# Eight rounding steps of GpSimd moved from ahead of a split of row maxima to behind it

## The chip, the cores and the metric

One core of one Trainium2 chip runs the whole program. The metric is the time of one execution on the device in microseconds, as the median of three runs. Five engines take part: TensorE (PE in the rows, PEld for its weight loads), VectorE (DVE), ScalarE (ACT), GpSimd (POOL) and SyncE (SP), which only issues transfers here.

## What is computed

The input is x with 4 x 1024 tokens of 128 features. The output is x plus an attention block plus a feed-forward block, both of which read the same layer norm of x:

```python
xn = _layernorm(x, axis=-1)
x = x + attn(xn, Wq, bq, Wk, bk, Wv, bv, Wo, bo) + ffn(xn, w_gate, w_up, w_down)
# attn: 16 heads of 8 features, a linear bias per head on the scores, softmax over 1024 keys
# ffn:
gate = fp4_linear(x, w_gate)
y = fp4_linear(x, w_up)
h = jax.nn.silu(gate) * y
return fp4_linear(h, w_down)
```

`fp4_linear` rounds both its operands to a grid of eight magnitudes in blocks of 16 values, each block scaled by its largest magnitude over 6. The feed-forward width is 352.

## The kernel before

**Tiling.** The attention goes in 32 halves m: 4 batches x 4 quads of heads x 2 halves of the queries. A half takes 8 units, so the main loop has 256 units U (and 16 more that drain it). In a unit, TensorE makes four score products for the exponentials (`score`, L1247, 128 keys x 512 queries each) and, for a later half, four score products the other way round (`half_chunk`, L1228, 128 queries x 512 keys each), out of which VectorE takes the row maxima (L1079). The maxima run ahead of the exponentials by `LEAD` = 22 chunks of two such products. ScalarE takes the exponentials (L863); TensorE multiplies them by the values (`value_product`, L1258).

**The way of the maxima.** When the last chunk of a half has been reduced, VectorE joins the two halves of each row into `neg_max` (L1085). GpSimd splits it into two bf16 parts (`max_parts`, L759 and L760) and raises `parts_max_ok` (L762). TensorE transposes the parts (`turn`, L1236), ScalarE keeps them (L869), SyncE writes them to DRAM and reads them into the operand rows of the scores (L536, L539), and the scores of the half begin three units after the transposition. The transposition of half m stands at the end of unit 8m - 3 (`turn_unit`), and GpSimd's split at the head of the same unit. VectorE's `neg_max` for it comes at the end of unit 8m - 4.

**The rounding.** The feed-forward block goes in 16 pairs p of token tiles, one every 15 units. Its places are given by a small planner (`plan`), and the rounding of its hidden values is tied to `up`, the unit of the pair's last `up` product. It is split into steps:

- VectorE: block maxima, scales (`up` + 3) and their inverses (`up` + 4, L1063)
- GpSimd, `scale_to_grid` at `up` + 5: two multiplications (L633, 128 x 704, and L635, 128 x 256), then `z_ok`
- VectorE, `powers` at `up` + 6, second half of the unit: waits for `z_ok`, one operation (L1068), then `pow_ok`
- GpSimd, `add_power` at `up` + 7: waits for `pow_ok`, two operations (L644 and L645, 128 x 960)
- GpSimd, `take_power` at `up` + 9: one operation (L650)
- GpSimd, `scale_back` at `up` + 10: two operations (L661 writes `hq`, L669 writes `xq`), then `quant_ok`

TensorE transposes `hq` (job `hT`, L1288) 13 or 14 units after `up` and again later, after a wait for `quant_ok`.

**Order.** Each engine has its own program, in which all of this is written in the order of units; an engine does nothing out of that order. Inside a unit GpSimd's order is: the split of the maxima, the bias, the attention result (`context`, L749), jobs of the feed-forward block (`swish` L722 and L723, `hidden` L728, `add_down` L735, `add_wo` L741), the steps of the rounding, the normalisation and the three-part split of q and k. TensorE's banks for row maxima are three, so it can be at most three products ahead of VectorE; its banks for everything that ScalarE empties are four.

Of the kernel before, what the change touches and what calls it, by code (L numbers as in the profile page):

```python
# [74 lines left out]
HALVES = 2 * B * QUADS  # L75
# [5 lines left out]
def turn_unit(m):  # L81
    return (16 * m + 15 - LEAD) // 2 + 1
# [25 lines left out]
def head(U, j):  # L108
# [6 lines left out]
FROM_XT = {("gate", 0): 2, ("gate", 1): 4, ("up", 0): 7, ("up", 1): 9, ("hT", 0): 23, ("hT", 1): 26,  # L115
           ("down", 0): 28, ("down", 1): 31}
ROUNDED = 13


def norm_unit(b):  # L120
    return 1 if b == 1 else 60 * b - 59


def parts_unit(g):
    return 60 * (g // 2 - 1) + 16 + 15 * (g % 2)


def plan():
# [17 lines left out]
    for p in range(NP):  # L146
        start = FFN_FIRST + FFN_STEP * p
        U = put(start, "xT", p)
        for kind, t in FROM_XT:
            U = U + (ROUNDED if (kind, t) == ("hT", 0) else 1)  # L150
            if p + 1 < NP or kind in ("gate", "up"):
# [74 lines left out]
def attn_ffn(nc, x, wq, bq, wk, bk, wv, bv, wo, bo, wg, wu, wd, out):  # L226
    with ExitStack() as ctx:
# [352 lines left out]
        def _(pool):  # L580
# [48 lines left out]
            def scale_to_grid(job):  # L629

                pool.wait_ge(inv_ok, job + 1)
                w, values = (W_END, w_all) if job == 0 else (PI, hid)
                mark(nc.gpsimd.tensor_tensor(blocks(zb[:, 0:w]), blocks(values[:]), spread(inv[:, 0:w // BLK]), ALU.mult))  # L633
                for c, p in x_cols(job):
                    mark(nc.gpsimd.tensor_tensor(blocks(zb[:, c:c + PW]), blocks(pair_x(p)),  # L635
                                                 spread(inv[:, c // BLK:(c + PW) // BLK]), ALU.mult))
                settle()
                pool.sem_inc(z_ok, 1)

            def add_power(job):  # L640
                w = job_cols(job)
                z, m = zb[:, 0:w], mb[:, 0:w]
                pool.wait_ge(pow_ok, job + 1)
                link(nc.gpsimd.tensor_scalar(m, m, 1.0, ROUND, ALU.max, ALU.mult))  # L644
                link(nc.gpsimd.tensor_tensor(z, z, m, ALU.add))  # L645

            def take_power(job):
                w = job_cols(job)
                z, m = zb[:, 0:w], mb[:, 0:w]
                link(nc.gpsimd.tensor_tensor(z, z, m, ALU.subtract))  # L650

            def scale_back(job):

                if job == 0:
                    mark(nc.gpsimd.tensor_tensor(blocks(w_all[:]), blocks(zb[:, 0:W_END]), spread(sc[:, 0:W_END // BLK]),
                                                 ALU.mult))
                else:
                    n = PI // BLK
                    if job >= 2:
                        pool.wait_ge(st_full, ST["hT", job - 2, 1] + 1)  # L660
                    mark(nc.gpsimd.tensor_tensor(  # L661
                        hq[:, :, 0:I].rearrange("p t (n k) -> p t n k", k=BLK),
                        zb[:, 0:PI].rearrange("p (t n k) -> p t n k", t=2, k=BLK),
                        sc[:, 0:n].rearrange("p (t n) -> p t n", t=2).unsqueeze(3).to_broadcast([P, 2, n // 2, BLK]),
                        ALU.mult))
                for c, p in x_cols(job):
                    if p >= 2:
                        pool.wait_ge(st_full, ST["xT", p - 2] + 1)
                    mark(nc.gpsimd.tensor_tensor(blocks(xq[p % 2][:]), blocks(zb[:, c:c + PW]),  # L669
                                                 spread(sc[:, c // BLK:(c + PW) // BLK]), ALU.mult))  # L670
                settle()
                pool.sem_inc(quant_ok, 1)
# [12 lines left out]
            def add_bias(b):  # L685

                pool.wait_ge(bo_ok, 1)
                for i in range(2):
                    group = x_s[:, b * S + i * GW:b * S + (i + 1) * GW].rearrange("p (t e) -> p t e", e=E)
                    ins = nc.gpsimd.tensor_tensor(group, group, bo_s[:].unsqueeze(1).to_broadcast([P, GT, E]), ALU.add)  # L690
                ins.then_inc(xb_ok, 1)
# [27 lines left out]
            def swish(p):  # L719

                pool.wait_ge(st_free, ST["gate", p, 1] + 1)
                link(nc.gpsimd.tensor_scalar(tanh_s[:], tanh_s[:], 1.0, None, ALU.add))  # L722
                link(nc.gpsimd.tensor_tensor(gate_s[:], tanh_s[:], gate_s[:], ALU.mult))  # L723

            def hidden(p, t):
                half = slice(t * I, (t + 1) * I)
                pool.wait_ge(st_free, ST["up", p, t] + 1)
                link(nc.gpsimd.tensor_tensor(hid[:, half], gate_s[:, half], up_s[:, half], ALU.mult))  # L728
                pool.sem_inc(hid_ok, 1)

            def add_down(p, t):
                to = x_s[:, p * PW + t * P:p * PW + (t + 1) * P]
                pool.wait_ge(st_free, ST["down", p, t] + 1)
                pool.wait_ge(xb_ok, p // 4 + 1)
                link(nc.gpsimd.tensor_tensor(to, to, down_s[:, t * P:(t + 1) * P], ALU.add))  # L735
                pool.sem_inc(down_ok, 1)

            def add_wo(hb, i):
                to = o_s[hb % 2][:, i * PW:(i + 1) * PW]
                pool.wait_ge(st_free, ST["wo", hb, i] + 1)  # L740
                nc.gpsimd.tensor_tensor(to, to, x_s[:, hb * GW + i * PW:hb * GW + (i + 1) * PW], ALU.add).then_inc(out_ok, 1)  # L741

            def context(m):
                b, quad, half = m // 8, m // 2 % QUADS, m % 2
                pool.wait_ge(pv_r_ok, m + 1)
                heads = pv_s[:].rearrange("p (t h c) -> p t h c", h=4, c=32)
                if b >= 2 and quad == 0 and half == 0:
                    pool.wait_ge(st_full, ST["ctxT", 2 * b - 3] + 1)
                nc.gpsimd.tensor_tensor(  # L749
                    ctx_s[b % 2][:, 4 * half:4 * half + 4, 32 * quad:32 * quad + 32].rearrange(  # L750
                        "p t (h d) -> p t h d", d=D), heads[:, :, :, 0:D],
                    pv_r[:].rearrange("p (t h) -> p t h", h=4).unsqueeze(3).to_broadcast([P, 4, 4, D]),
                    ALU.mult).then_inc(ctx_ok, 1)

            def max_parts(m):
                pool.wait_ge(max_ok, m + 1)
                if m >= 2:
                    pool.wait_ge(st_full, ST["turn", m - 2] + 1)
                link(nc.gpsimd.tensor_copy(neg_parts[m % 2][:, 0:16], neg_max[m % 2][:]))  # L759
                link(nc.gpsimd.tensor_tensor(neg_parts[m % 2][:, 16:32], neg_max[m % 2][:], neg_parts[m % 2][:, 0:16],  # L760
                                             ALU.subtract))
                pool.sem_inc(parts_max_ok, 1)  # L762
# [8 lines left out]
            for U in range(NU + 2 * KT):  # L771
                b, u = divmod(U, QUADS * UNITS)
                for m in range(1, HALVES):
                    if U == turn_unit(m):
                        max_parts(m)
                if u == 2 and b < B:
                    add_bias(b)
                for job in JOBS.get(U - 1, ()):
                    if job[0] == "pvT":
                        context(job[1])  # L780
                for job in JOBS.get(U - 1, ()):
                    if job[0] == "gate" and job[2] == 1:
                        swish(job[1])
                    elif job[0] == "up":
                        hidden(job[1], job[2])
                    elif job[0] == "down":
                        add_down(job[1], job[2])
                    elif job[0] == "wo" and job[1] + 1 < NG:
                        add_wo(job[1], job[2])
                for p in range(NP):  # L790
                    up = AT["up", p, 1]
                    if U == up + 5:
                        scale_to_grid(p + 1)
                    if U == up + 7:
                        add_power(p + 1)
                    if U == up + 9:
                        take_power(p + 1)
                    if U == up + 10:
                        scale_back(p + 1)
                for g in range(2, NG):  # L800
                    if U == norm_unit(g // 2):
                        normalize(g)
                    if U == parts_unit(g):
                        three_parts(g, 0, "q")
                    if U == parts_unit(g) + 2:
                        three_parts(g, 1, "k")
# [600 lines left out]
```

## Time and profile before

| | |
|---|---|
| median of 3 runs | 804.6 us (804.46 to 805.57) |
| the profiled execution, its own time | 801.33 us |
| its span, first to last instruction | 799.5 us |
| TensorE busy | 92% |
| VectorE busy | 89% |
| ScalarE busy | 83% |
| GpSimd busy | 53% |
| granted TensorE clock, mean | 0.97 |

A unit takes some 2.8 to 3 us. Three engines are nearly full and hand banks to each other, so the table alone doesn't say what sets the time: the waits and the chain of work have to be read at the places of the change.

### The profile page before, as it was taken

To read this page: it belongs to the slowest core of one execution; us is meant where nothing else is said; L and a number is where in the kernel's file an instruction comes from. 1 tells how busy PE (TensorE), PEld (TensorE's weight loads), DVE (VectorE), ACT (ScalarE), POOL (GpSimd) and SP (SyncE) were. 2 spreads that over 40 slices of the span, in tenths; PEclk is the share of its full clock that TensorE was granted. 3 is DMA by queue.
4 is the path that set the end of the run, shared out by engine and by line. 5 is a ranking of instruction groups with operands and counts; after the bars stand their busy time and mean duration, and the time that the engine had idled before them with its cause. 6 is when DMAs were issued, how large, how long until landed. Compare 5 with 4: busy or idle time off the path is not lost.

```text
span 799.5 us, 14573 instructions
## 1 busy us (share of the span) xinstructions
PE 736.7 (92%) x4951; PEld 218.3 (27%) x4951; DVE 711.9 (89%) x1304; ACT 661.4 (83%) x1366; POOL 427.0 (53%) x449
## 2 busy tenths in 40 slices
PE   6399998999899999999999999999899999999987
PEld 2012222222223222322222332322222322222223
DVE  8998899999899899999999899999898999999930
ACT  4107988888888988898889989898888898898896
POOL 5792157563545658581736656662627372634351
PEclk9657999999999999999999999999999999999999
DMA  6730002041101020060101001240100100000000
GB/s 183 219 73 2 2 3 81 2 134 27 41 1 41 2 81 2 23 151 15 42 1 42 3 33 50 93 93 2 41 2 22 34 3 1 15 2 2 2 2 27
DMA packets 33042, 31.90 MB, mean 40 GB/s; under 512 B 4456, under 2 KB 26856, under 8 KB 32968
## 3 DMA queue, kind: packets, MB, share of 16 engines
q1 hardware_dynamic: 32840, 30.86, 14.3%
q8 instruction: 40, 0.66, 0.4%
q14 instruction: 34, 0.28, 0.1%
q10 hardware_dynamic: 128, 0.10, 0.0%
HBM read 15.91 MB, written 15.04 MB: 39 GB/s over the span
## 4 chain that ended last, share of the span: by engine, by line
PE 63%; DVE 25%; ACT 5%; POOL 4%; issue 3%; DMA 0%; POOLq 0%; SPq 0%; ACTq 0%; DVEq 0%
PE pv L1258 23%; PE mx L1228 23%; DVE neg_half L1079 20%; ACT probs L863 3%; PE low L1281 3%; PE low L1275 2%; PE low L1307 2%; PE low L1296 2%; PE low L1208 2%; POOL zb L645 1%; PE low L1288 1%; PE low L1322 1%; POOL mb L644 1%; DVE am L1048 1%; PE low L1204 1%
## 5 line engine op out<-in xcount | busy, mean ns | idle before, releaser
L1079 DVE TENSOR_REDUCE neg_half<-mx 128x1 f32<-128x512 f32 x1024 | 641.4, 683 | 50.9 <-PE mx L1228 46.0
L863 ACT ACTIVATE probs<-low 128x512 f32<-128x512 f32 x1006 | 549.9, 616 | 61.8 <-PE low L1247 52.1
L1228 PE MATMUL mx<-k_op,q_op 51*128 51x512 bf16 x1024 | 325.8, 394 | 40.1 <-DVE neg_half L1079 28.3
L1247 PE MATMUL low<-q_op,k_op 53*128 53x512 bf16 x1006 | 305.6, 384 | 0.0
L1258 PE MATMUL pv<-probs,v_op 128*32 128x512 f32 x2048 | 273.6, 606 | 3.4 <-ACT pv_s L961 1.4
L1228 PEld LDWEIGHTS mx<-k_op,q_op 51*128 51x128 bf16 x1024 | 68.7, 94 | 333.0 <-DVE neg_half L1079 285.9
L749 POOL TENSOR_TENSOR ctx_s<-pv_s,pv_r 128x128 f32<-128x128 f32 x32 | 13.0, 406 | 127.2 <-DVE pv_r L1097 126.9
L644 POOL TENSOR_SCALAR mb<-mb 128x960 f32<-128x960 f32 (+2 forms) x17 | 58.7, 3455 | 36.7 <-DVE mb L1068 36.3
L1247 PEld LDWEIGHTS low<-q_op,k_op 53*128 53x128 bf16 x1006 | 66.0, 94 | 7.4 <-ACT probs L863 6.1
L1258 PEld LDWEIGHTS pv<-probs,v_op 128*32 128x32 f32 x2048 | 40.3, 108 | 88.6 <-ACT probs L863 41.2
L728 POOL TENSOR_TENSOR hid<-gate_s,up_s 128x352 f32<-128x352 f32 x32 | 29.9, 935 | 51.8 <-ACT up_s L890 51.1
L735 POOL TENSOR_TENSOR x_s<-x_s,down_s 128x128 f32<-128x128 f32 x32 | 14.6, 455 | 57.1 <-ACT down_s L896 55.0
L650 POOL TENSOR_TENSOR zb<-zb,mb 128x960 f32<-128x960 f32 (+2 forms) x17 | 38.2, 2246 | 2.5 <-POOL x_s L735 1.1
L645 POOL TENSOR_TENSOR zb<-zb,mb 128x960 f32<-128x960 f32 (+2 forms) x17 | 38.2, 2247 | 1.4
L759 POOL CAST neg_parts<-neg_max 128x16 bf16<-128x16 f32 x31 | 6.8, 220 | 52.3 <-DVE neg_max L1085 43.3
L869 ACT COPY max_t<-low 32x128 bf16<-32x128 bf16 x32 | 8.2, 256 | 32.1 <-PE low L1236 31.6
L722 POOL TENSOR_SCALAR tanh_s<-tanh_s 128x704 f32<-128x704 f32 x16 | 31.7, 1979 | 2.7 <-POOL xq L669 1.6
L920 ACT COPY pv_s<-low 128x512 f32<-128x512 f32 x31 | 18.2, 587 | 14.0 <-PE low L1307 14.0
L633 POOL TENSOR_TENSOR zb<-hid,inv 128x704 f32<-128x704 f32 x16 | 22.2, 1385 | 13.7 <-DVE inv L1063 12.8
L1097 DVE RECIPROCAL pv_r<-pv_s 128x16 f32<-128x16 f32 x32 | 7.9, 246 | 24.0 <-ACT pv_s L920 24.0
L1296 PE MATMUL low<-dT_s,hqT 128*128 128x128 f32 x186 | 29.0, 292 | 0.0
L723 POOL TENSOR_TENSOR gate_s<-tanh_s,gate_s 128x704 f32<-128x704 f32 x16 | 26.9, 1682 | 1.3
(162 smaller groups left out, 658.7 us busy)
## 6 DMA issues: line engine op xcount, KB each, us to landing
q_op<-q_rows SPq DMA_DIRECT2D x30, 192.0 KB, 3.9
k_op<-k_rows SPq DMA_DIRECT2D x30, 192.0 KB, 4.8
q_rows<-qp SPq DMA_DIRECT2D x8, 384.0 KB, 2.6
k_rows<-kp SPq DMA_DIRECT2D x8, 384.0 KB, 3.2
x_s<-in_L_attn_inputs_dram SPq DMA_DIRECT2D x8, 256.0 KB, 3.8
q_rows<-qp SPq DMA_DIRECT2D x8, 256.0 KB, 3.0
k_rows<-kp SPq DMA_DIRECT2D x8, 256.0 KB, 3.1
out_dram<-o_s SPq DMA_DIRECT2D x7, 256.0 KB, 2.3
```

Of the source, the lines that this page charges most:

```text
L644: link(nc.gpsimd.tensor_scalar(m, m, 1.0, ROUND, ALU.max, ALU.mult))
L645: link(nc.gpsimd.tensor_tensor(z, z, m, ALU.add))
L650: link(nc.gpsimd.tensor_tensor(z, z, m, ALU.subtract))
L722: link(nc.gpsimd.tensor_scalar(tanh_s[:], tanh_s[:], 1.0, None, ALU.add))
L723: link(nc.gpsimd.tensor_tensor(gate_s[:], tanh_s[:], gate_s[:], ALU.mult))
L728: link(nc.gpsimd.tensor_tensor(hid[:, half], gate_s[:, half], up_s[:, half], ALU.mult))
L863: nc.scalar.activation(probs[U % 3][:, 2 * g + x, :], bank("exp", U, j), ACT.Exp).then_inc(st_free, 1)
L1079: nc.vector.tensor_reduce(neg_half[m % 2][:, i + kh:i + kh + 1], slot("max", pos, kh), AX.X, ALU.max, negate=True).then_inc(mx_free, 1)
L1228: nc.tensor.matmul(slot("max", pos, kh), q, k, start=True, stop=True).then_inc(mx_full, 1)
L1247: nc.tensor.matmul(bank("exp", U, j), k_op[quad][r, g, kt * P:(kt + 1) * P], q_op[quad][r, g, half * HALF:(half + 1) * HALF], start=True, ...
L1258: ins = nc.tensor.matmul(pv[32 * hh:32 * hh + 32, :], v_op[b % 2][:, kt, 4 * quad + hh, :], probs[U % 3][:, hh, :], start=(kt == 0), stop= ...
L1296: ins = nc.tensor.matmul(bank("down", p, t)[:, 0:P], hqT[t][0:n, c * P:(c + 1) * P], dT_s[0:n, c * P:(c + 1) * P], start=(c == 0), stop=(c ...
```

## The change

A rounding step of GpSimd that falls in a unit directly ahead of a transposition of maxima is written one unit later, and so stands behind the split of the maxima on GpSimd instead of ahead of it. Nothing is added or removed, and no other engine's program is touched.

```diff
+def step_unit(U):
+    return U + 1 if U + 1 in [turn_unit(m) for m in range(1, HALVES)] else U
...
-                    if U == up + 5:
+                    if U == step_unit(up + 5):
                         scale_to_grid(p + 1)
-                    if U == up + 7:
+                    if U == step_unit(up + 7):
                         add_power(p + 1)
-                    if U == up + 9:
+                    if U == step_unit(up + 9):
                         take_power(p + 1)
-                    if U == up + 10:
+                    if U == max(step_unit(up + 10), step_unit(up + 9)):
                         scale_back(p + 1)
```

Of the 64 steps of the main loop eight move: `scale_to_grid` of pairs 0 and 8 (units 20 and 140, now 21 and 141, halves 3 and 18), `add_power` of pairs 2 and 10 (52 and 172, now 53 and 173, halves 7 and 22), `take_power` of pairs 4 and 12 (84 and 204, now 85 and 205, halves 11 and 26) and `scale_back` of pairs 5 and 13 (100 and 220, now 101 and 221, halves 13 and 28). In the changed kernel the lines of these functions are 5 higher.

**First place: GpSimd's program in units 50 to 54, pair 2 and half 7.** `mb` and `zb` are the buffers of the rounding, `neg_parts1` the split maxima, `x_s` the sum that `add_down` adds to. Before:

```order
L749 TENSOR_TENSOR ctx_s0<-pv_s,pv_r 128x4x32
L644 TENSOR_SCALAR mb<-mb 128x960
L645 TENSOR_TENSOR zb<-zb,mb 128x960
L759 CAST neg_parts1<-neg_max1 128x16
L760 TENSOR_TENSOR neg_parts1<-neg_max1,neg_parts1 128x16
L735 TENSOR_TENSOR x_s<-x_s,down_s 128x128
L650 TENSOR_TENSOR zb<-zb,mb 128x960
```

and with the change:

```order
L754 TENSOR_TENSOR ctx_s0<-pv_s,pv_r 128x4x32
L764 CAST neg_parts1<-neg_max1 128x16
L765 TENSOR_TENSOR neg_parts1<-neg_max1,neg_parts1 128x16
L740 TENSOR_TENSOR x_s<-x_s,down_s 128x128
L649 TENSOR_SCALAR mb<-mb 128x960
L650 TENSOR_TENSOR zb<-zb,mb 128x960
L655 TENSOR_TENSOR zb<-zb,mb 128x960
```

The two operations of `add_power` stood ahead of the split and now stand behind it, and behind the addition as well.

**Second place: GpSimd's program in units 19 to 22, pair 0 and half 3.** `hid` and `xn_s0` are the values to be rounded. Before:

```order
L749 TENSOR_TENSOR ctx_s0<-pv_s,pv_r 128x4x32
L633 TENSOR_TENSOR zb<-hid,inv 128x704
L635 TENSOR_TENSOR zb<-xn_s0,inv 128x256
L759 CAST neg_parts1<-neg_max1 128x16
L760 TENSOR_TENSOR neg_parts1<-neg_max1,neg_parts1 128x16
L644 TENSOR_SCALAR mb<-mb 128x960
```

and with the change:

```order
L754 TENSOR_TENSOR ctx_s0<-pv_s,pv_r 128x4x32
L764 CAST neg_parts1<-neg_max1 128x16
L765 TENSOR_TENSOR neg_parts1<-neg_max1,neg_parts1 128x16
L638 TENSOR_TENSOR zb<-hid,inv 128x704
L640 TENSOR_TENSOR zb<-xn_s0,inv 128x256
L649 TENSOR_SCALAR mb<-mb 128x960
```

The two multiplications whose end raises `z_ok` now follow the split.

**Third place: GpSimd's program in units 99 to 104, pair 5 and half 13.** Before:

```order
L741 TENSOR_TENSOR o_s1<-o_s1,x_s 128x256
L661 TENSOR_TENSOR hq<-zb,sc 128x2x352
L669 TENSOR_TENSOR xq1<-zb,sc 128x256
L759 CAST neg_parts1<-neg_max1 128x16
L760 TENSOR_TENSOR neg_parts1<-neg_max1,neg_parts1 128x16
L722 TENSOR_SCALAR tanh_s<-tanh_s 128x704
L723 TENSOR_TENSOR gate_s<-tanh_s,gate_s 128x704
```

and with the change:

```order
L746 TENSOR_TENSOR o_s1<-o_s1,x_s 128x256
L764 CAST neg_parts1<-neg_max1 128x16
L765 TENSOR_TENSOR neg_parts1<-neg_max1,neg_parts1 128x16
L727 TENSOR_SCALAR tanh_s<-tanh_s 128x704
L728 TENSOR_TENSOR gate_s<-tanh_s,gate_s 128x704
L666 TENSOR_TENSOR hq<-zb,sc 128x2x352
L674 TENSOR_TENSOR xq1<-zb,sc 128x256
```

`scale_back` now stands behind the split and behind both operations of `swish`.

## Rows read from the trace of the kernel before

**Rows 1.** The page's first part: busy us (share of the span) and instructions
```profile
PE 736.7 (92%) x4951; PEld 218.3 (27%) x4951; DVE 711.9 (89%) x1304; ACT 661.4 (83%) x1366; POOL 427.0 (53%) x449
```

**Rows 2.** Waits, whole span: who waited for whom, us in total, times, longest
```profile
PEld mx L1228 <- DVE neg_half L1079: 285.9, 441, 4.6
...
PE low L1236 <- POOLq L762: 6.8, 7, 1.7
```

**Rows 3.** The page's groups: busy us, mean ns, idle before and its releaser
```profile
L1079 DVE TENSOR_REDUCE neg_half<-mx 128x1 f32<-128x512 f32 x1024 | 641.4, 683 | 50.9 <-PE mx L1228 46.0
```

**Rows 4.** TensorE's timeline, transpositions of maxima (start, duration, idle before)
```profile
193.25 0.22 PE L1236 MATMUL low<-ident_b,neg_parts 128*32 128x128 bf16 x1
...
217.49 0.22 PE L1236 MATMUL low<-ident_b,neg_parts 128*32 128x128 bf16 x1 [1.68 <-POOLq L762]
...
239.80 0.22 PE L1236 MATMUL low<-ident_b,neg_parts 128*32 128x128 bf16 x1
...
564.81 0.22 PE L1236 MATMUL low<-ident_b,neg_parts 128*32 128x128 bf16 x1 [1.67 <-POOLq L762]
```

**Rows 5.** The timeline of all engines around half 7's transposition
```profile
213.34 0.19 DVE L1085 TENSOR_REDUCE neg_max<-neg_half 128x16 f32<-128x32 f32 x1
...
214.75 1.07 PE L1258 MATMUL pv<-probs,v_op 128*32 128x512 f32 x8
...
217.54 0.45 POOL L735 TENSOR_TENSOR x_s<-x_s,down_s 128x128 f32<-128x128 f32 x1 [0.24 <-POOL neg_parts L760]
...
218.06 5.11 DVE L1079 TENSOR_REDUCE neg_half<-mx 128x1 f32<-128x512 f32 x8 [2.14 <-PE mx L1228]
```

**Rows 6.** The chain of work that ended last, around half 7's transposition
```profile
211.00 3.42 POOL mb L644
214.50 2.24 POOL zb L645
...
217.07 0.23 POOL neg_parts L760
```

**Rows 7.** The timeline around half 3's transposition, where `scale_to_grid` of pair 0 moves
```profile
123.11 0.62 POOL L635 TENSOR_TENSOR zb<-xn_s,inv 128x256 f32<-128x256 f32 x1
...
124.05 0.19 DVE L1085 TENSOR_REDUCE neg_max<-neg_half 128x16 f32<-128x32 f32 x1
...
124.30 0.20 POOL L759 CAST neg_parts<-neg_max 128x16 bf16<-128x16 f32 x1 [0.57 <-PE low L1247]
...
124.58 0.22 POOL L760 TENSOR_TENSOR neg_parts<-neg_max,neg_parts 128x16 bf16<-128x16 f32 x1
...
126.54 0.65 DVE L1068 TENSOR_SCALAR mb<-zb 128x960 int32<-128x960 int32 x1
...
127.85 0.09 PEld L1228 LDWEIGHTS mx<-k_op,q_op 51*128 51x128 bf16 x1 [1.07 <-DVE neg_half L1079]
```

**Rows 8.** The timeline at the last pair, whose `powers` waited for `scale_to_grid`
```profile
766.97 1.39 POOL L633 TENSOR_TENSOR zb<-hid,inv 128x704 f32<-128x704 f32 x1 [0.18 <-POOL x_s L735]
...
768.43 0.53 DVE L1068 TENSOR_SCALAR mb<-zb 128x704 int32<-128x704 int32 x1 [2.57 <-POOLq L638]
```

**Rows 9.** The timeline around half 18's transposition, where `scale_to_grid` of pair 8 moves
```profile
470.72 0.22 POOL L760 TENSOR_TENSOR neg_parts<-neg_max,neg_parts 128x16 bf16<-128x16 f32 x1
...
472.87 0.65 DVE L1068 TENSOR_SCALAR mb<-zb 128x960 int32<-128x960 int32 x1
```

**Rows 10.** Timelines of GpSimd, VectorE and TensorE around half 13, where `scale_back` moves
```profile
353.99 1.39 POOL L661 TENSOR_TENSOR hq<-zb,sc 128x704 f32<-128x704 f32 x1
...
354.45 0.19 DVE L1085 TENSOR_REDUCE neg_max<-neg_half 128x16 f32<-128x32 f32 x1
...
356.88 1.98 POOL L722 TENSOR_SCALAR tanh_s<-tanh_s 128x704 f32<-128x704 f32 x1 [0.20 <-ACT probs L863]
358.94 1.68 POOL L723 TENSOR_TENSOR gate_s<-tanh_s,gate_s 128x704 f32<-128x704 f32 x1
...
362.92 0.55 PE L1288 MATMUL low<-ident,hq 128*128 128x128 f32 x3
```

## Prediction

> **What bounds the kernel now.** I began with the busy shares [rows 1]. TensorE, VectorE and ScalarE are all above 80%, GpSimd is at 53%. By shares alone no edit of GpSimd's program should matter. The waits say more [rows 2]. TensorE waits 286 us in 441 pieces for VectorE's row maxima, so the two go in step. But seven times, 6.8 us in all, TensorE stood at the transposition of maxima because GpSimd had not yet raised `parts_max_ok`. These waits are what the change can touch, so I read each transposition in TensorE's timeline. Two of the waits are at places where a step is moved: half 7, 1.68 us, and half 22, 1.67 us [rows 4]. The other five (together 6.8 - 3.35 = 3.45 us) are at halves 9, 12, 15, 24 and 30, where no step moves. At the other six places of the change (halves 3, 11, 13, 18, 26, 28) TensorE has no such wait.
>
> Does such a wait reach the end? Two views say yes. The chain of work that ended last, which elsewhere runs through TensorE and VectorE, goes through GpSimd here: `add_power`'s two operations and then the split [rows 6]. And VectorE goes empty too, for 2.14 us [rows 5]. Nor is it made good later: from half 6 to half 7 the transpositions are 24.24 us apart, from half 7 to half 8 22.31 us [rows 4]. VectorE's own 32 reductions in eight units take 32 x 0.683 = 21.9 us [rows 3], so the stretch behind the wait is near its floor, and the one with the wait, less 1.68, would be 22.56 us, still above it.
>
> **The change, part by part.** No instruction is added and no transfer moves; SyncE, which issues them all, keeps its program. Only GpSimd's order differs, at eight places of four kinds.
>
> *`add_power`, halves 7 and 22: the gain.* Before, `add_power` starts at 211.00 and takes 3.42 + 2.24 us, and the split follows it, though VectorE had `neg_max` ready at 213.34 + 0.19 = 213.53 [rows 5, 6]. With the split first, it starts 0.25 us after the start of `neg_max` (124.05 to 124.30), its second half 0.28 us later (124.58) [rows 7], and GpSimd is free 0.47 us after that (217.07 to 217.54) [rows 5, 6]: 213.59, 213.87, 214.34. `parts_max_ok` is thus up by 214.3. TensorE then comes to the transposition when its value products end, 214.75 + 1.07 = 215.82 [rows 5], instead of 217.49. That is 1.67 us, and half 22's wait is of the same size. What is late next is VectorE: of its gap of 2.14 us 2.14 - 1.67 = 0.47 stays, since TensorE's next product of maxima follows the transposition anyway. I take 1.68 + 1.67 = 3.35 us. The bounds are nothing, if another wait fills the hole, and VectorE's whole gap, 2 x 2.14 = 4.3 us. I take the value near the upper end, since chain and gap agree on the place.
>
> `add_power` itself starts behind the split and `add_down` (0.45 us [rows 5]), near 214.9, 3.9 us later than 211.00. It ends near 220.6; `take_power` (as long as L645, 2.2 us) and `scale_back` (1.39 + 0.62 us [rows 7, 8]) end near 225. `hq` is wanted in unit 59, five and a half units of 2.8 us (22.31 / 8) after the transposition at 215.82, that is near 231. The cover is some 6 us, so this costs nothing.
>
> *`scale_to_grid`, halves 3 and 18: a new wait.* Here the change moves work that VectorE waits for, and by little slack. Half 3: the split's second operation starts at 124.58 [rows 7]; the multiplications start 0.43 to 0.47 us later, at 125.03, and take 1.39 [rows 8] + 0.62 [rows 7], to 127.04. At the last pair `powers` began 768.43 - (766.97 + 1.39) = 0.07 us after such an end [rows 8], so here at 127.1 at the latest. Before it began at 126.54 [rows 7]. VectorE stands for about 0.5 us, with its next reduction queued behind `powers`. TensorE was itself waiting for that reduction at 127.85 [rows 7], so the 0.5 us pass on in full. Half 18: 470.72 + 0.45 + 1.39 + 0.62 + 0.07 = 473.25 against 472.87 [rows 9], 0.4 us. The sum is 0.9 us; the operations overlap their records by some 0.05 us, so I take 0.8. The bounds are nothing, if ScalarE or TensorE would have been late by as much, and 1.6 us, twice this.
>
> GpSimd's durations carry this term. The Trainium skill, Perfetto Trace Analysis, on the GPSIMD instruction's lifecycle, says that a span of this engine in the profile is not to be relied on and that the spacing of starts should be used. The gap between the two kinds of reading here is about 0.05 us at each place, so by spacing alone the sum would be 0.1 us lower.
>
> *`take_power`, halves 11 and 26.* It starts behind the split, some 2.5 us later than before, and `scale_back` with it. Its taker, the transposition of `hq`, stands three and a half units, 10 us, behind. Nothing.
>
> *`scale_back`, halves 13 and 28.* TensorE did not wait for the split, so nothing is gained. `scale_back` is now behind `swish`: `neg_max` at 354.45, split from 354.70 to 355.43, `swish` for 358.94 - 356.88 + 1.68 and the 0.2 us that GpSimd takes between dependent operations, 3.94 us, to 359.37, `scale_back` 1.39 + 0.62, to 361.4. TensorE takes `hq` at 362.92 [rows 10]. The cover is 1.5 us, thin but there; half 28 repeats the pattern. Nothing.
>
> **The sum.** -3.35 + 0.8 = -2.55 us. The profiled execution took 801.33 us for a span of 799.5, so it would take 798.8. The median shown is 804.6, 3.3 us above that execution, and I let that distance stand: 804.6 - 2.6 = **802.0 us**. About 0.2% (1.6 us) is what a measurement of this kernel can tell from no change.
>
> **The rivals.**
> - *The hole is filled.* TensorE, VectorE and ScalarE are all near full, and with the wait gone one of the other two may be late in the units after it. For it: busy shares of 83 to 92%. Against it: the chain and the 22.31 us. If half of the gain goes this way, -1.7 + 0.8 gives 803.7 us, no change that can be told. The Trainium skill has this as a rule: Perfetto Trace Analysis, Identifying the Most-Contended Engine, would have the fullest engine worked on first, and GpSimd is the emptiest. By that rule alone the time would stay at 804.6; the waits [rows 2] already speak against it. Chance 0.17.
> - *The new wait costs nothing.* If `powers` is not late, because VectorE comes to it later than before, the full 3.35 us show: 801.2 us. For it: at half 18 TensorE isn't waiting for VectorE at that moment. Chance 0.13.
> - *The thin cover tears.* `scale_back` behind `swish` ends after TensorE wants `hq`, at halves 13 and 28. Then TensorE stands in front of everything queued behind that transposition. It decides from 1.5 us of extra lateness, and outweighs the gain only when both are late by a further 1.3 us and more, say 2.2 us each: -2.55 + 4.4 gives 806.4 us. For it: only 1.5 us of cover [rows 10], and `swish` also waits for ScalarE. Against it: ScalarE's part was done before, since `swish` started at once. Chance 0.07.
> - *The change doesn't reach the waits.* If the split is late for another reason at halves 7 and 22, all that is left is the 0.8 us: 805.4 us. The split waits for `neg_max`, which was there 3.3 us before it began [rows 5, 6], so this is unlikely. Chance 0.03.
>
> **How the numbers follow.** The forecast has 0.60, and its own range is 801.0 to 803.0. Range for 8 in 10: down to 800.7, which takes in the full gain without the new wait and a little of VectorE's larger gap; up to 803.8, which takes in the hole half filled. Faster by over 0.2% (below 803.0): 0.60 + 0.13 and a little of the first rival, 0.75. Within 0.2%: 0.17. Slower: the torn cover and a little more, 0.08.
>
> **What would show it.** In the changed kernel's waits, TensorE's wait at the transposition for GpSimd should be near 3.4 us in five pieces. The transpositions of halves 6 and 7, and of 21 and 22, should be near 22.6 us apart, with VectorE's gap there near 0.5 us. `powers` of pairs 0 and 8 should show a wait for GpSimd of 0.5 and 0.4 us, and halves 3 to 4 and 18 to 19 be longer by that. The transpositions of `hq` of pairs 5 and 13 should show no wait for GpSimd. I am wrong if those show one, if the reductions behind halves 7 and 22 wait in more places than before, or if the five waits left grow.

## The result, and the profile after

The changed kernel took 797.19 us (median of 5, 796.64 to 800.1), the kernel before beside it 804.55 us (801.03 to 805.57, 5): ratio 0.9929, 95% interval 0.9908 to 0.9951. A repeat later, with more executions, gave 798.19 against 803.44 us, ratio 0.9927, interval 0.9901 to 0.9952. The ratio is the estimate that its interval belongs to, taken over all executions of both kernels, and not the quotient of the two medians (which is 0.9909 here). By the ratio 5.7 us were gained, by these two medians 7.4, by those of the repeat 5.3. The forecast of 802.0 us, a ratio of 0.9968, had the sign right and the size too small: some 6 us were gained, not 2.6, and its range ended at 800.7.

The profiled execution of the changed kernel took 800.1 us for a span of 798.3. That is only 1.2 us under the profiled one of before, so the two traces alone don't show the 6 us. First what they do show. The waits of the changed kernel (engine and line, what was waited for, us in total, times, longest; line numbers from 120 on are 5 higher than before):

```profile
DVE neg_half L1084 <- PE mx L1233: 42.2, 113, 1.5
...
PE low L1241 <- POOLq L767: 3.5, 5, 1.1
...
DVE mb L1073 <- POOLq L643: 3.2, 3, 2.6
...
PE mx L1252 <- DMA q_op<-m_rows: 2.3, 1, 2.3
```

TensorE's wait for GpSimd fell from 6.8 us in seven pieces [rows 2] to 3.5 in five. VectorE's idle time behind TensorE fell from 46.0 us [rows 3] to 42.2. `powers` now waits for `scale_to_grid` in three places instead of one. TensorE's timeline (start, duration) has these transpositions of maxima, of halves 6, 7, 8, 21, 22 and 23:

```profile
193.80 0.22 PE L1241 MATMUL low<-ident_b,neg_parts 128*32 128x128 bf16 x1
...
216.17 0.22 PE L1241 MATMUL low<-ident_b,neg_parts 128*32 128x128 bf16 x1
...
238.48 0.22 PE L1241 MATMUL low<-ident_b,neg_parts 128*32 128x128 bf16 x1
...
539.11 0.22 PE L1241 MATMUL low<-ident_b,neg_parts 128*32 128x128 bf16 x1
...
561.70 0.22 PE L1241 MATMUL low<-ident_b,neg_parts 128*32 128x128 bf16 x1
...
584.01 0.22 PE L1241 MATMUL low<-ident_b,neg_parts 128*32 128x128 bf16 x1
```

From 6 to 7 it is 22.37 us instead of 24.24 [rows 4], and from 21 to 22 22.59 instead of 24.45 (before: 540.36 to 564.81). The gain is 1.87 + 1.86 = 3.73 us, and the stretch behind is 22.31 as before. Around half 7 the timeline shows why:

```profile
213.87 0.19 DVE L1090 TENSOR_REDUCE neg_max<-neg_half 128x16 f32<-128x32 f32 x1
...
216.74 3.78 DVE L1084 TENSOR_REDUCE neg_half<-mx 128x1 f32<-128x512 f32 x6 [0.28 <-PE mx L1233]
```
```profile
214.13 0.20 POOL L764 CAST neg_parts<-neg_max 128x16 bf16<-128x16 f32 x1 [3.89 <-DVE neg_max L1090]
...
215.51 3.42 POOL L649 TENSOR_SCALAR mb<-mb 128x960 f32<-128x960 f32 x1 [0.20 <-POOL x_s L740]
```

GpSimd stands ready 3.89 us ahead of the split, takes it 0.26 us after `neg_max` starts, and does `add_power` behind it. VectorE's gap is 0.28 us instead of 2.14 [rows 5]. The price stands at halves 3 and 18:

```profile
127.09 0.66 DVE L1073 TENSOR_SCALAR mb<-zb 128x960 int32<-128x960 int32 x1 [0.39 <-POOLq L643]
...
471.64 0.66 DVE L1073 TENSOR_SCALAR mb<-zb 128x960 int32<-128x960 int32 x1 [0.21 <-POOLq L643]
```

The turns behind them grew by 0.49 us (22.15 to 22.64) and 0.29 us (22.64 to 22.93), 0.78 in all. Half 13 gave 0.20 us. The last transposition is at 763.41 instead of 766.55: -3.14 us, as the sum -3.73 + 0.78 - 0.20 = -3.15 has it.

Behind it 1.9 us are lost again. The chain of work that ended last shows the last row maxima on their way through memory, and TensorE's timeline the wait for them:

```profile
764.68 3.53 DMA m_rows<-max_t
768.74 1.66 DMA q_op<-m_rows
```
```profile
770.45 0.39 PE L1252 MATMUL mx<-q_op,k_op 53*128 53x512 bf16 x1 [2.28 <-DMA q_op<-m_rows]
```

Before, this transfer landed 1.37 us after its issue (at 767.82) and TensorE waited 0.34 us. The step-by-step terms held, then, but the pair of traces hides a gain, and shows a loss that the four other executions of the changed kernel leave no room for (part 6).

### The profile page after: what moved, and what is told of

It is laid out like the page before. It is cut to its first block, busy times and chain, and to the rows that moved or that the text cites. A ratio compares the mean times of both kernels' runs of the same rounds, so it can differ in the third digit from the quotient of the medians.

```text
span 798.3 us, 14574 instructions
## 1 busy us (share of the span) xinstructions
PE 736.3 (92%) x4951; PEld 218.1 (27%) x4951; DVE 711.7 (89%) x1304; ACT 659.8 (83%) x1366; POOL 426.9 (53%) x449
## 4 chain that ended last, share of the span: by engine, by line
PE 65%; DVE 24%; ACT 4%; POOL 3%; issue 2%; DMA 1%; SPq 0%; POOLq 0%; ACTq 0%; DVEq 0%
PE pv L1263 24%; PE mx L1233 23%; DVE neg_half L1084 19%; PE low L1280 3%; PE low L1286 3%; PE low L1312 2%; PE low L1301 2%; ACT probs L868 2%; PE low L1213 2%; PE low L1293 1%; PE low L1327 1%; DVE am L1053 1%; PE low L1209 1%; DVE stats L996 1%; PE low L1199 1%
## 5 line engine op out<-in xcount | busy, mean ns | idle before, releaser
L1084 DVE TENSOR_REDUCE neg_half<-mx 128x1 f32<-128x512 f32 x1024 | 640.7, 680 | 47.3 <-PE mx L1233 42.2
L638 POOL TENSOR_TENSOR zb<-hid,inv 128x704 f32<-128x704 f32 x16 | 22.2, 1386 | 12.0 <-DVE inv L1068 10.8
```

The costliest lines, as they stand in the source:

```text
L1084: nc.vector.tensor_reduce(neg_half[m % 2][:, i + kh:i + kh + 1], slot("max", pos, kh), AX.X, ALU.max, negate=True).then_inc(mx_free, 1)
```

## Experiments

Times are medians; "before" is the kernel before, measured beside the others. The kernels were measured in several groups and on three chips, each group beside the kernel before, so ratios, not times, compare between groups. A turn is the distance between the transpositions of two halves, read from TensorE's timeline. Except where said, the experiments change only which of the four steps stand one unit later.

**1. The parts of the change.** Each kernel has the changed kernel's text with some of the four steps at their old units, for instance for `add_power` alone:

```diff
-                    if U == step_unit(up + 5):
+                    if U == up + 5:
                         scale_to_grid(p + 1)
                     if U == step_unit(up + 7):
                         add_power(p + 1)
-                    if U == step_unit(up + 9):
+                    if U == up + 9:
                         take_power(p + 1)
...
```

None moved:

> Control: all eight steps stand back in their old units, so GpSimd's order is that of the kernel before. Theory A (the steps explain some 3 us, the rest of the measured 7 us is the spread between executions, from a transfer in the drain that lands late in some of them): 0 us against before, with single executions near 801 and near 804.5 us. Theory B (the whole 7 us belongs to the moved steps): also 0 us, but all executions near 804.5 us; those near 801 would be rare.

Measured 803.52 us, before 803.57, ratio 0.9989 (0.9974 to 1.0004): the order of before takes the time of before. The executions lie all over 801.1 to 804.9 us, not in two groups. All moved:

> The changed kernel again, beside the control on one chip. Theory A: the main loop up to the last transposition of maxima is 3.1 us shorter than in the control's profile, in any execution; times in two groups some 3 us apart, and the difference of the medians depends on how many fall in each group: -3 to -7 us. Theory B: -7 us again, and a profile of a fast execution shows a second place that is shorter, outside the eight places of the change.

Measured 798.7 us, ratio 0.9929 (0.9904 to 0.9953). From the first transposition of maxima to the last it is 6.2 us shorter than with none moved, not 3.1, and the turns behind halves 7 and 22 make the difference: a second place, as theory B has it. `add_power` alone:

> Only add_power of pairs 2 and 10 moves (halves 7 and 22). Theory A: the distances of the transpositions 6 to 7 and 21 to 22 fall from 24.24 and 24.45 us to 22.4 and 22.6, nothing else moves, the loop is 3.7 us shorter than the control's. No wait of powers for GpSimd except at the last pair. In time 0.7 us faster than with all eight. Theory B: as much as all eight, since it's the earlier loop that shifts the transfers.

Measured 797.28 us, ratio 0.9919 (0.9888 to 0.995). Five of the six executions lie between 796.3 and 798.1 us, one at 803.59 with a mean clock of 0.963, though it has neither of the two holes; no profile shows where that one lost its time. `scale_to_grid` alone:

> Only scale_to_grid of pairs 0 and 8 moves (halves 3 and 18). Theory A: two new waits of powers of some 0.3 us each, the distance 3 to 4 grows by 0.5 us and 18 to 19 by 0.3 us, the loop is 0.8 us longer than the control's, time +0.8 us. Theory B (a shift of any sort changes which transfer is late): time changes by some us in either direction though the loop is 0.8 us longer.

Measured 804.63 us, ratio 1.0013 (0.999 to 1.0036), with turns 3 to 4 and 18 to 19 longer by 0.49 and 0.28 us. The other two, `take_power` and `scale_back`:

> take_power and scale_back alone are moved, at halves 11 and 26, 13 and 28. Prediction: nothing at all four. The trace of the whole change hints at 0.2 us at half 13 (turn 12 to 13 shorter by 0.20). So turn distances as in the order of before but for that one, and the time of the kernel before less 0.2, no measurable difference.

Measured 803.27 us, ratio 1.0004 (0.9984 to 1.0024), and in the trace the turn 12 to 13 at 22.71 instead of 22.91 us. All of the gain that the times show belongs to `add_power`, which alone is worth 6.3 us, not the 3.7 of its two turns. The loss by `scale_to_grid` and the 0.2 us of `scale_back` are shown by the turns; in the times they are too small to tell from nothing.

**2. One program, two kinds of execution.** The profile of the order of before, taken anew, told where the rest was. This is the kernel before itself once more:

> The kernel before, for one more profile of the same program. Clock theory: of its holes at halves 7 and 22 each is followed by a stretch at granted clock 0.50 (turns 7 to 8 or 22 to 23 longer by 1.5 us or more), or the execution is one of the shorter ones, near 801, with both distances at 22.3. The span should equal the first profile's 799.5 plus what these two distances, the start and the landing of the last row maxima add, within 0.3 us.

It took 802.53 us, for a span of 800.7; by the sum in its expectation the span should be 799.5 + 1.52 + 1.22 - 1.45 = 800.8. Its transpositions of halves 6, 7 and 8:

```profile
191.80 0.22 PE L1236 MATMUL low<-ident_b,neg_parts 128*32 128x128 bf16 x1
...
216.04 0.22 PE L1236 MATMUL low<-ident_b,neg_parts 128*32 128x128 bf16 x1 [1.68 <-POOLq L762]
...
239.87 0.22 PE L1236 MATMUL low<-ident_b,neg_parts 128*32 128x128 bf16 x1
```

The turn with the hole is 24.24 us, as in rows 4, but the one behind it is 23.83, where rows 4 have 22.31. The windows of 1 us show TensorE's granted clock (window, its length, busy share and instruction count of PE, PEld, DVE, ACT, POOL, then PEclk, DMA share, GB/s):

```profile
216.00:217.00 1.00, 0.96 (x7) 0.30 (x7) 0.39 (x1) 0.55 (x2) 0.73 (x2) 1.00 0.00 0
217.00:218.00 1.00, 0.65 (x8) 0.20 (x10) 1.00 (x3) 1.00 (x3) 1.00 (x1) 0.67 0.07 16
218.00:219.00 1.00, 1.00 (x8) 0.10 (x8) 1.00 (x2) 0.77 (x2) 0.94 (x1) 0.50 0.00 0
219.00:220.00 1.00, 1.00 (x6) 0.13 (x4) 0.10 (x1) 0.00 (x0) 0.98 (x1) 0.50 0.02 7
220.00:221.00 1.00, 1.00 (x5) 0.27 (x2) 0.59 (x1) 0.50 (x2) 0.98 (x2) 0.62 0.00 1
```

Between 1 and 2 us after the end of the hole the clock falls from 2.4 to 1.2 GHz (0.50) for some 3 us. TensorE stays busy, and VectorE, at 0.10 in the fourth window, starves. The first profile of before has 1.00 in every window from 213 to 232 us and from 561 to 580:

```profile
217.00:218.00 1.00, 0.51 (x5) 0.30 (x7) 0.00 (x0) 0.26 (x1) 0.67 (x2) 1.00 0.00 0
218.00:219.00 1.00, 0.65 (x8) 0.10 (x2) 0.94 (x2) 0.85 (x2) 0.83 (x1) 1.00 0.04 8
219.00:220.00 1.00, 1.00 (x10) 0.16 (x8) 1.00 (x3) 1.00 (x3) 1.00 (x1) 1.00 0.03 8
```

The changed kernel, which has no hole there, has 1.00 too:

```profile
218.00:219.00 1.00, 1.00 (x10) 0.11 (x4) 1.00 (x3) 0.90 (x2) 0.94 (x1) 1.00 0.03 8
219.00:220.00 1.00, 1.00 (x6) 0.30 (x2) 0.99 (x3) 0.67 (x2) 0.98 (x1) 1.00 0.01 4
```

Five profiles have both holes open: before, its repeat, none moved, `scale_to_grid` alone, and `take_power` with `scale_back`. Of their ten holes eight are followed by such a stretch; only the two of the profile that the prediction was made from are not. The stretch is some 3 us long in seven cases and some 7 us in one, behind half 22 with `scale_to_grid` alone. The turn behind is longer by 1.52 and 1.22, 1.57 and 1.53, 1.60 and 2.92, 1.54 and 1.43 us in these four, 1.7 us a hole in the mean of the eight and 1.3 in the mean of all ten. The executions without a profile agree in kind. Beside this repeat the kernel before ran from 800.73 us at a mean clock of 0.970 to 807.45 us at 0.961, while the changed kernel had 0.972 in four of its first five. Those of before at 0.961 to 0.964 are below the 0.968 of the profiles with two short stretches, so by the clock they had more than these; where, no profile shows.

**3. Holes kept, TensorE kept busy in them.** To part the clock from everything else, the order of before got matmuls whose results are overwritten:

```diff
+                for _ in range(26 if m in (7, 22) else 0):
+                    nc.tensor.matmul(bank("turn", m)[:, 0:P], ident_b[:], ident_b[:], start=True, stop=True)
                 nc.tensor.wait_ge(parts_max_ok, m + 1)
```

> The order of the kernel before, with 26 matmuls of 128 columns on TensorE (about 1.5 to 2 us) ahead of its wait for the split at halves 7 and 22; their results are overwritten by the transposition. Clock theory (the hole of the kernel before is followed by a stretch at the lower clock in its typical executions): the holes stay in the turns, so 6 to 7 and 21 to 22 stay near 24.3 us, but no stretch of granted clock 0.50 follows, 7 to 8 and 22 to 23 stay at 22.3, and the time is 2.5 to 3 us under the kernel before in the same call, about 801. Rival (what the prediction left out is not the clock behind the hole but something else in the program's position): the time of the kernel before, 804, within 0.5 us.

Measured 800.28 us, before 802.85, ratio 0.997 (0.9956 to 0.9985). The timeline:

```profile
193.31 0.22 PE L1243 MATMUL low<-ident_b,neg_parts 128*32 128x128 bf16 x1
...
215.81 1.62 PE L1241 MATMUL low<-ident_b 128*128 128x128 bf16 x26
217.47 0.23 PE L1243 MATMUL low<-ident_b,neg_parts 128*32 128x128 bf16 x1
...
239.80 0.22 PE L1243 MATMUL low<-ident_b,neg_parts 128*32 128x128 bf16 x1
```

The hole is as long as ever (24.16 us to half 7), the turn behind is 22.33, and the clock stays up behind the hole:

```profile
218.00:219.00 1.00, 0.65 (x8) 0.10 (x2) 0.94 (x2) 0.85 (x2) 0.82 (x2) 1.00 0.04 8
219.00:220.00 1.00, 1.00 (x10) 0.16 (x8) 1.00 (x3) 1.00 (x3) 1.00 (x1) 1.00 0.03 8
```

All twelve executions had a mean clock of 0.970 to 0.972 and lay within 1.7 us, where those of before spread over 5. GpSimd, VectorE and the semaphores do what they did before; some 2.5 us went by idle filling alone.

**4. Holes made where there were none.** The kernel with `add_power` alone got delays on GpSimd ahead of the split at four quiet halves, and then the filling as well:

```diff
                 pool.wait_ge(max_ok, m + 1)
+                if m in (4, 19, 27, 29):
+                    for _ in range(11):
+                        link(nc.gpsimd.memset(idle_s[:], 0.0))
                 if m >= 2:
                     pool.wait_ge(st_full, ST["turn", m - 2] + 1)
```

> add_power alone moved, and eleven small memsets on GpSimd (about 2.9 us together) ahead of the split at halves 4, 19, 27 and 29, where nothing waited. Holes of about 1.7 us should open at these four transpositions. If a hole costs its width alone: 4 x 1.7 = 7 us over the kernel with add_power alone, near 804. Clock theory: the clock falls to 0.50 behind some of them, 1.5 to 2.9 us each on top, near 807 to 812.

Measured 815.57 us, ratio 1.0161 (1.0136 to 1.0186). That is above even the upper expectation, and the width alone (near 804) is ruled out.

> The same four holes with 26 matmuls of 128 columns on TensorE ahead of its wait at each. Clock theory: only the width is left, about 7 us over the kernel with add_power alone, near 804, and 3 to 8 us under the unfilled one; no stretch of clock 0.50 behind the four. Rival (TensorE's idle time has no part in it, only GpSimd's delay): the same as unfilled within 1 us.

Measured 805.67 us, ratio 1.0042 (1.0026 to 1.0058), 9.9 us under the unfilled kernel where the rival had 1 us at most. Transpositions 3 to 5 without the filling, then the windows behind the hole at half 4:

```profile
126.12 0.22 PE L1245 MATMUL low<-ident_b,neg_parts 128*32 128x128 bf16 x1
...
150.46 0.22 PE L1245 MATMUL low<-ident_b,neg_parts 128*32 128x128 bf16 x1 [2.00 <-POOLq L771]
...
174.37 0.22 PE L1245 MATMUL low<-ident_b,neg_parts 128*32 128x128 bf16 x1
```
```profile
151.00:152.00 1.00, 1.00 (x4) 0.30 (x2) 0.97 (x2) 0.88 (x2) 0.37 (x1) 0.84 0.04 8
152.00:153.00 1.00, 1.00 (x5) 0.13 (x4) 0.55 (x2) 0.86 (x3) 0.24 (x1) 0.50 0.00 0
153.00:154.00 1.00, 1.00 (x10) 0.20 (x8) 1.00 (x3) 0.89 (x2) 0.77 (x2) 0.50 0.02 4
```

And with it:

```profile
125.44 0.22 PE L1247 MATMUL low<-ident_b,neg_parts 128*32 128x128 bf16 x1
...
149.70 0.23 PE L1247 MATMUL low<-ident_b,neg_parts 128*32 128x128 bf16 x1 [0.35 <-POOLq L771]
...
172.17 0.22 PE L1247 MATMUL low<-ident_b,neg_parts 128*32 128x128 bf16 x1
```
```profile
152.00:153.00 1.00, 1.00 (x12) 0.16 (x6) 1.00 (x3) 0.80 (x2) 0.82 (x1) 1.00 0.01 4
```

The turns with the holes are longer by 8.45 us in the one and 8.1 us in the other. The turns behind are longer by 1.38, 1.59, 2.61 and 1.48 us without filling (7.1 us) and by none with it. The holes came out at 1.8 to 2.0 us rather than 1.7, and the fillings left 0.2 to 0.35 us of them idle. The profiles differ by 10.8 us of span, of which 7.1 is this, 2.7 lie behind the last transposition (part 6), and the rest is the start and the widths.

**5. Smaller holes, and fewer.** Seven memsets instead of eleven:

> As the kernel with four new holes, but seven memsets instead of eleven ahead of the split at halves 4, 19, 27 and 29, so that the holes are about 0.95 us wide (seven of 0.26 us less the 0.87 us of slack that the wider ones left). If the clock answers to a hole of any width: 4 x 0.95 + 4 x 1.5 to 2.6 us over the kernel with add_power alone, 807 to 811. If holes this narrow pass without it, as the five that were there before did in the profiles: the width alone, 3.8 us, near 801.

Measured 802.67 us, ratio 0.9998 (0.9972 to 1.0024). In the profile (800.42 us) the holes are 0.5 to 0.74 us, the turns with them 0.7 to 0.94 longer (3.4 us in all), and no stretch at a lower clock follows. Of the turns behind, only 29 to 30 is longer, by 0.29 us, since the wait at half 30 grew from 0.44 to 0.73 us. So in this profile small holes cost little but their width. The median is another matter. The profiled execution is 2.3 us faster than it, and by the ratios this kernel is 6 us slower than that with `add_power` alone, not 3.7. Three of the twelve executions were above 806 us at a mean clock of 0.963. The 807 to 811 us of a fall behind every hole are ruled out, but that small holes are free of it in all executions isn't shown: whether the slower ones lost their time behind these holes or elsewhere no profile shows.

Fewer holes come of setting the split ahead of `add_power` two units away too, and ahead of `swish` one unit away. The other three steps stand at their old units, and the old call of `swish` in the loop over the jobs is taken out:

```diff
-                    if U == step_unit(up + 7):
+                    if U == behind_split(up + 7, 2):
                         add_power(p + 1)
...
+                for p in range(NP):
+                    if U == behind_split(AT["gate", p, 1] + 1, 1):
+                        swish(p)
```

> add_power alone is moved, now also where the split is two units behind it (halves 9 and 24), and the swish step is set behind the split of halves 15 and 30. The waits for the split at halves 9, 15, 24 and 30 (0.54, 1.02, 1.09, 0.44 us) should go, only the 0.4 us of half 12 stays. If each hole is worth its width and nothing else: 3.1 us under the kernel with add_power alone, near 794.2. If the steps that stand later cost a wait elsewhere (the powers of a pair, GpSimd's chain behind them): 795.5 to 797.

Measured 794.91 us, ratio 0.9915 (0.989 to 0.9939). That lies between the two outcomes expected, nearer to the first. The turns 8 to 9, 14 to 15, 23 to 24 and 29 to 30 are 0.72, 1.22, 1.29 and 0.62 us shorter than with `add_power` alone: 3.85 us for 3.1 us of waits. The five waits are down to one:

```profile
PE low L1245 <- POOLq L770: 0.4, 1, 0.4
```

Since its ratio was hardly better than that of `add_power` alone, it was run again beside the changed kernel:

> The changed kernel once more. With the removed holes and the clock behind them the sum is -3.15 us in the turns (3.73 gained at halves 7 and 22, 0.2 at half 13, 0.78 paid at 3 and 18) and about -3 us of clock: ratio 0.992 to 0.993. In the profile both turns behind halves 7 and 22 are 22.3 us; the last row maxima land either in 1.4 us or in about 3.5 us, which adds 1.9 us to the profiled time.

> The kernel with the split ahead at seven halves, beside the changed kernel on one chip. Its turns were 3.85 us shorter than those of add_power moved alone in the profiles, and that one saves the 0.78 us of scale_to_grid too: if turns are all, it is 4 us under the changed kernel. If the smaller holes were now and then followed by the lower clock, it is more; if the clock falls elsewhere in it instead (its executions had a lower mean clock, 0.961 to 0.971), 2 us or less.

The changed kernel took 798.19 us, this one 795.29 us, ratios to before 0.9927 and 0.9894 (0.9866 to 0.9923). Its best execution, 792.86 us, lies 3.9 us under the changed kernel's best, 796.75: the turns' 4 us show there; the medians differ by 2.9. The intervals of the two overlap, so that it beats the kernel before is shown by the times, that it beats the changed one by the turns only.

**6. The last row maxima.** The late landing came back in the profiles of all moved (3.47 us), of the changed kernel's repeat (3.11), of `scale_to_grid` alone (3.42) and of the four new holes (3.11). In the other ten it took 1.37 us. With `scale_to_grid` moved it was late four times of four; once it was late without. In the two longest kernels (`scale_to_grid` alone and the four new holes) the hole it makes, 2.4 and 2.0 us, is again followed by a clock of 0.50. There it took 36.9 and 36.5 us from the last transposition to the end, where the three other late profiles have 34.6 to 34.9 and nine of the ten on time 32.7 to 33.0. It is not in most executions of the changed kernel's first measurement. By an estimate from the turns the kernel must be 0.6 us slower than `add_power` alone (fastest execution 796.28), so with 1.9 us on top an execution would hardly be under 798.8; four of the five took 796.6 to 797.2. In its repeat and with all moved, six of eleven executions without a profile took 798.1 us or more, and how many of them had it no profile shows. What makes it late wasn't found: `scale_to_grid` of the last pair stands at its old place in all of them. A packet of the queue that fetches instructions came 1.0 to 1.5 us after the issue in all five late profiles, but in eight of the ten others too, so that alone doesn't do it.

## Why the prediction was wrong

- **The hole's width** (3.35 us). Measured 3.73. VectorE's gap shrank by 1.86 us rather than by the predicted 1.67. The choice near the upper bound was right.
- **The new wait** (0.8 us for bounds of 0 and 1.6). Measured 0.78, by 0.49 and 0.29. The waits themselves are 0.39 and 0.21 us. The rival that it costs nothing is refuted.
- **`take_power` at nothing.** Right: halves 11 and 26 show no difference.
- **`scale_back` at nothing.** Nearly: 0.20 us gained at half 13, also where these two steps alone were moved. Before, the split ended at 356.47 + 0.22 = 356.69 and the transposition began at 356.88. It had followed the split closely there, in a wait too short to have a row of its own. The thin cover held: `hq` was ready at 357.91 + 1.38 = 359.29, and TensorE took it at 361.41.
- **"The chain and the gap agree", and the stretch behind the hole is "near its floor".** This held in the one execution that I read: the turns behind the holes are 22.31 us with and without them, so the rival that the hole is filled is refuted. The step that failed is the last one of the sum: *"The median shown is 804.6, 3.3 us above that execution, and I let that distance stand."* I added the distance on both sides and didn't ask what it consisted of. The gain of `add_power` thus held the hole's width alone, and what a hole costs behind it stood in the sum at nothing. Most of the distance was the very thing that the change removes: the clock's fall behind the two holes, 2.7, 3.0, 3.1 and 4.5 us in the four other profiles with both holes, the last in the slowest execution of `scale_to_grid` alone. (The first profile of before also started later, by 0.7 to 1.5 us at half 1's transposition than three of them, which hid a part of that distance; and 804.6 is itself 1.0 to 1.7 us above the later medians of before, 802.85 to 803.57.) So a hole of 1.68 us cost 1.87 us of width and, where the clock fell, some 1.7 us more behind. Over all five profiles the fall costs 2.7 us in the mean, and the sum with it is -3.15 - 2.7 = -5.8 us, from the 803.5 us of the order of before to 797.7, a ratio of 0.9928. Measured were ratios of 0.9929, 0.9927 and, for all moved, 0.9929. Filling the two holes gave back 2.6 us by the medians, about the same amount by another way.
- **The range** (800.7 to 803.8) had a lower end made of unknowns within the traced execution only. The distance of 3.3 us between trace and median should have stood in it as a thing that the change might take away.

The granted clock stood in the windows of the trace, but at 1.00, so it gave no warning; the median did. The Trainium skill (TensorE: Matmul & The Clock Gate, Why this matters for your kernels) wants no long idle gaps of TensorE between bursts of matmuls, since the clock goes back to its lower level behind them. The direction agrees with eight holes of ten here. The gaps it names are longer than these holes, though; by its figure these holes would have cost nothing beyond their width, and the 1.2 to 2.9 us measured behind holes of 1.7 us decide against that.

## What to carry over

An idle hole of TensorE is to be priced at its width plus the slower stretch that can follow it, and one profile in which the clock held is no proof that it does. Where the profiled execution is faster than the median by more than the spread of one kind of execution, ask what the median's extra time is before carrying it over unchanged; a second profile of the same program answers it. Where the hole itself can't be closed, overwritten matmuls in it keep the clock and were worth 2.5 us here. Behind smaller holes, of 0.4 to 1.1 us, no profile shows a fall, but the spread of the executions leaves open that they are sometimes followed by one.

## What was not expected of the hardware

In four of the five profiles with both holes open, TensorE, idle for 1.7 us and then busy again at 2.4 GHz for 0.6 to 2.1 us (worked out from the windows), was granted 0.50 for some 3 us, though it stayed busy; in the fifth, of the same program as one of the four, it kept 1.00. With `scale_to_grid` alone the stretch behind half 22 was some 7 us (568 to 575 us). In the kernel with four new holes the clock once fell within the first microsecond behind the hole, and also stayed down for some 7 (684 to 691 us). And the same small transfer, at the same place in the program, landed after 1.37 us in ten profiles and after 3.1 to 3.5 us in five, its cause still open.
